# A four-pass recurrent scan on one core: the state update moves from VectorE to ScalarE, with VectorE writing the input line into PSUM ahead of the products

## What is computed

```python
def step(w, b):
    def f(carry, inp):
        nxt = inp + _conv1d(carry, w, b)   # 5 taps, 48 -> 48 channels, along the line
        return (nxt, nxt)
    return f
_, d_rest = scan(step(down_w, down_b), d0, xs[1:])            # D: rows downwards
seq = concatenate([D[Hh - 3::-1], D[Hh - 1:Hh]], 0)
_, u_rest = scan(step(down_w, down_b), u0, seq)               # U: rows upwards, input one line ahead
_, r_rest = scan(step(right_w, right_b), r0, ws[1:])          # R: columns to the right
_, l_rest = scan(step(left_w, left_b), l0, R[Ww - 2::-1])     # L: columns to the left
x = x + L(_gn(x))
```

## Time and profile before

| what | value |
|---|---|
| median of 3 runs | 2966.16 us (2957.53 to 2975.64) |
| the profiled execution, its own time | 2969.76 us |
| its span | 2968.0 us |
| TensorE's granted clock over the span | 0.935 of full |
| TensorE matmul, busy | 2535.7 us (85%) |
| VectorE busy | 1454.5 us (49%) |
| ScalarE busy | 824.4 us (28%) |
| GpSimd busy | 250.2 us (8%) |
| first layer's scan | 980.7 to about 1694 us |
| second layer's scan | about 1797 to 2514 us |

### The profile page before, as it was taken

The page is one execution under the profiler, slowest core; times in us unless marked ns, Lnnn a source line. Parts: engine busy times, 40 slices in busy tenths (PEclk is TensorE's granted clock), DMA queues, the critical chain, the costliest instruction groups (busy, mean ns, idle before and its releaser), DMA issues.

```text
span 2968.0 us, 46070 instructions
## 1 busy us (share of the span) xinstructions
PE 2535.7 (85%) x18068; PEld 2198.1 (74%) x18068; DVE 1454.5 (49%) x3029; ACT 824.4 (28%) x1353; POOL 250.2 (8%) x244
## 2 busy tenths in 40 slices
PE   2989999999999899999999807999999998005786
PEld 2989849849844899999999807999999998002343
DVE  3323233233222555545555674555455556776665
ACT  3433353353356101440024420014400244002221
POOL 1000000000000720000000140000000000344110
PEclk9999999999999899999999958999999999557888
DMA  8830000012002300000000092000000000573222
GB/s 150 148 62 1 1 0 1 1 28 58 1 0 64 65 1 1 1 1 1 1 1 1 12 270 60 1 1 1 1 1 1 1 1 1 178 276 98 85 85 85
DMA packets 51629, 129.81 MB, mean 44 GB/s; under 512 B 9120, under 2 KB 34048, under 8 KB 44896
## 3 DMA queue, kind: packets, MB, share of 16 engines
q1 hardware_dynamic: 48352, 113.92, 15.8%
q10 hardware_dynamic: 2976, 13.34, 1.5%
q0 software_dynamic: 128, 0.01, 0.0%
HBM read 76.91 MB, written 50.33 MB: 43 GB/s over the span
## 4 chain that ended last, share of the span: by engine, by line
PE 83%; DMA 6%; DVE 6%; issue 2%; ACT 1%; POOL 1%; SPq 0%; DVEq 0%; ACTq 0%; POOLq 0%
PE bank L939 18%; PE bank L940 15%; PE bank L941 15%; PE bank L848 13%; PE bank L902 11%; PE bank L863 3%; PE bank L853 3%; DMA flat_rows<-work 2%; PE bank L976 2%; DVE work L316 2%; DMA work<-saved 1%; PE bank L1034 1%; DMA work<-in_x 1%; PE bank L967 1%; DMA saved<-image 1%
## 5 line engine op out<-in xcount | busy, mean ns | idle before, releaser
L1220 DVE SCALAR_TENSOR_TENSOR image<-bank,scan_bias,image 112x128 f32<-112x128 f32 x2032 | 781.8, 385 | 653.3 <-PE bank L941 650.4
L939 PE MATMUL bank<-image,scan_wt 112*112 112x128 f32 x4064 | 852.8, 291 | 32.1 <-ACT image L689 25.5
L940 PE MATMUL bank<-image,scan_wt 112*112 112x126 f32 x4064 | 771.3, 271 | 0.0
L941 PE MATMUL bank<-image,scan_wt 112*112 112x126 f32 x4064 | 770.0, 270 | 0.0
L939 PEld LDWEIGHTS bank<-image,scan_wt 112*112 112x112 f32 x4064 | 557.4, 175 | 65.3 <-ACT image L689 25.7
L940 PEld LDWEIGHTS bank<-image,scan_wt 112*112 112x112 f32 x4064 | 582.5, 176 | 0.0
L941 PEld LDWEIGHTS bank<-image,scan_wt 112*112 112x112 f32 x4064 | 578.8, 176 | 0.0
L848 PE MATMUL bank<-work 112*128 112x192 f32 x2304 | 423.7, 332 | 10.0 <-issue 10.0
L615 ACT ACTIVATE work<-image,gn_shift,gn_scale 48x567 f32<-48x567 f32 (+5 forms) x384 | 332.3, 898 | 345.5 <-PE bank L853 219.3
L707 ACT COPY work<-image 48x256 f32 (+1 forms) x256 | 105.8, 413 | 1041.8 <-PE bank L941 1041.3
L848 PEld LDWEIGHTS bank<-work 112*128 112x128 f32 x2304 | 375.0, 192 | 11.7 <-issue 11.2
(11 more groups left out here) (134 smaller groups left out, 1563.3 us busy)
## 6 DMA issues: line engine op xcount, KB each, us to landing
work<-saved SPq DMA_DIRECT2D x64, 384.0 KB, 8.5
saved<-image SPq DMA_DIRECT2D x10, 1536.0 KB, 20.7
flat_rows<-work ACTq DMA_DIRECT2D x32, 384.0 KB, 7.3
image<-flat_rows SPq DMA_DIRECT2D x4, 3072.0 KB, 13.9
out<-image SPq DMA_DIRECT2D x8, 1536.0 KB, 8.1
saved<-image SPq DMA_DIRECT2D x12, 768.0 KB, 9.5
band<-in_x SPq DMA_DIRECT2D x16, 384.0 KB, 5.5
work<-in_x SPq DMA_DIRECT2D x16, 384.0 KB, 5.5
```

The source lines that it names most:

```text
L939: mm(dst, wt[:, 1], src, start=True, stop=False)
L940: mm(dst[:, 1:J2, :], wt[:, 0], src[:, 0:J2 - 1, :], start=False, stop=False)
L941: mm(dst[:, 0:J2 - 1, :], wt[:, 2], src[:, 1:J2, :], start=False, stop=True).then_inc(s_prod[g], 1)
L1220: v.scalar_tensor_tensor(out=line(g, along_w, at), in0=prod, scalar=scan_bias[:, 3 * layer + kind:3 * layer + kind + 1], in1=line(g, along ...
```

## The change

- Each group now has two PSUM banks, used in turn (`state_bank(g, done)` is `bank[2 * g + done % 2]`).
- VectorE no longer updates the line. One step ahead it writes input line plus bias into the bank of the coming step (`preload`, a `tensor_scalar`), as soon as the state of two steps before has left that bank, and counts up `s_pre[g]`.
- TensorE's three products all have `start=False` and accumulate onto what VectorE wrote. Four products ahead of the first layer (`s_prime`) write the four banks once, so that later ones add.
- ScalarE waits for `s_pre[g]` of the next step and for `s_prod[g]`, copies the 112 x 128 sum from PSUM into the image line (`take_step`) and counts up `s_state[g]`. Its code is unrolled now.
- The exchanges go to VectorE (`swap_part`), single copies put behind the preloads: in passes U and L up to two in a step, three in every two steps, begun 5 or 3 steps late, the rest after the last preload of the pass.
- The counter `s_swap` starts at 0, so the waits for it in GpSimd and TensorE change by one.

```diff
+        def state_bank(g, done):
+            return bank[2 * g + done % 2][0:P, 0:2 * J2].rearrange("p (j q) -> p j q", q=2)
...
@@ scalar
-            def exchange(along_w, i, n):
...
-                own_wait(act, s_swap, n + 1)
-                nc.scalar.copy(swap_tmp[HI], part(LO, 1)).then_inc(s_swap, 1)
-                own_wait(act, s_swap, n + 2)
-                nc.scalar.copy(part(LO, 1), part(HI, 0)).then_inc(s_swap, 1)
-                own_wait(act, s_swap, n + 3)
-                nc.scalar.copy(part(HI, 0), swap_tmp[HI]).then_inc(s_swap, 1)
+            def take_step(layer, done, scan, n):
+                forward, along_w, _, _ = SCANS[scan]
+                _, at = step_at(forward, n)
+                for g in range(2):
+                    if n < STEPS - 1:
+                        act.wait_ge(s_pre[g], layer * PASSES * STEPS + done + 2)
+                    act.wait_ge(s_prod[g], layer * PASSES * STEPS + done + 1)
+                    nc.scalar.copy(line(g, along_w, at), state_bank(g, done)).then_inc(s_state[g], 1)
...
@@ tensor
                 for g in range(2):
+                    if n == 0:
+                        pe.wait_ge(s_pre[g], layer * PASSES * STEPS + done + 1)
                     pe.wait_ge(s_state[g], done + (layer * (PASSES * STEPS + 1) + 1))
                     src = line(g, along_w, at)
-                    dst = bank[g][0:P, 0:2 * J2].rearrange("p (j q) -> p j q", q=2)
-                    mm(dst, wt[:, 1], src, start=True, stop=False)
-                    mm(dst[:, 1:J2, :], wt[:, 0], src[:, 0:J2 - 1, :], start=False, stop=False)
-                    mm(dst[:, 0:J2 - 1, :], wt[:, 2], src[:, 1:J2, :], start=False, stop=True).then_inc(s_prod[g], 1)
+                    dst = state_bank(g, done)
+                    mm(dst, wt[:, 1], src, start=False, stop=False, skip_group_check=True)
+                    mm(dst[:, 1:J2, :], wt[:, 0], src[:, 0:J2 - 1, :], start=False, stop=False,
+                       skip_group_check=True)
+                    mm(dst[:, 0:J2 - 1, :], wt[:, 2], src[:, 1:J2, :], start=False, stop=True,
+                       skip_group_check=True).then_inc(s_prod[g], 1)
+            for i in range(4):
+                if i == 2:
+                    pe.wait_ge(s_sm_v, 5 * NB)
+                mm(bank[i][0:P, 0:2 * J2], group_half[:, :], identp[0:P, 0:2 * J2],
+                   start=True, stop=True).then_inc(s_prime, 1)
...
@@ vector
-            def step(layer, done, scan, n):
...
-                for g in range(2):
-                    dve.wait_ge(s_prod[g], done + (layer * PASSES * STEPS + 1))
-                    prod = bank[g][0:P, 0:2 * J2].rearrange("p (j q) -> p j q", q=2)
-                    v.scalar_tensor_tensor(out=line(g, along_w, at), in0=prod,
-                                           scalar=scan_bias[:, 3 * layer + kind:3 * layer + kind + 1],
-                                           in1=line(g, along_w, src), op0=ALU.add, op1=ALU.add).then_inc(s_state[g], 1)
+            def preload(layer, done, scan, n, g):
...
+                dve.wait_ge(s_state[g], layer * (PASSES * STEPS + 1) + 1 + max(done - 1, 0))
+                v.tensor_scalar(state_bank(g, done), line(g, along_w, src),
+                                scan_bias[:, 3 * layer + kind:3 * layer + kind + 1], None, ALU.add).then_inc(s_pre[g], 1)
+            def swap_part(along_w, i, m, n):
...
+                if n:
+                    dve.wait_ge(s_swap, n)
+                dst, src = ((swap_tmp[HI], part(LO, 1)), (part(LO, 1), part(HI, 0)), (part(HI, 0), swap_tmp[HI]))[m]
+                v.tensor_copy(dst, src).then_inc(s_swap, 1)
...
                 for scan in range(PASSES):
+                    lag = (None, 5, None, 3)[scan]
                     for n in range(STEPS):
-                        step(layer, scan * STEPS + n, scan, n)
+                        for g in range(2):
+                            preload(layer, done + n, scan, n, g)
+                            m = 2 * (n - lag) + g - 1 if lag else -1
+                            if m >= 0 and m % 4 < 3:
+                                swap_part(scan == 3, K2 - 1 - m // 4 - (scan == 1), m % 4, swaps)
+                                swaps += 1
+                    if lag:
+                        for g in range(2):
+                            dve.wait_ge(s_prod[g], layer * PASSES * STEPS + done + STEPS - 1)
+                        for i in ((K2 - 1,) if scan == 1 else ()) + (1,):
+                            for m in range(3):
+                                swap_part(scan == 3, i, m, swaps)
+                                swaps += 1
+                        for g in range(2):
+                            dve.wait_ge(s_state[g], layer * (PASSES * STEPS + 1) + 1 + done + STEPS)
+                        for m in range(3):
+                            swap_part(scan == 3, 0, m, swaps)
+                            swaps += 1
+                        dve.wait_ge(s_swap, swaps)
```

More of the change, by code:

```diff
@@ L249, in build @@
         s_state = [sem(f"s_state{g}") for g in range(2)]
+        s_pre = [sem(f"s_pre{g}") for g in range(2)]
+        s_prime = sem("s_prime")
         s_swap = sem("s_swap")
@@ L514, in _ @@
             pool.wait_ge(s_band, N_BAND)
[L516 removed]
+            pool.wait_ge(s_swap, 6 * K2)
             for g in range(2):
@@ L730, in _ @@
                 last.then_inc(s_tail, 1)
-                for g in range(2):
-                    act.wait_ge(s_prod[g], layer * PASSES * STEPS + 1)
-                n0 = layer * 2 * 3 * K2
-                prod0 = layer * PASSES * STEPS + STEPS
-                with act.Fori(0, K2 - 2) as i:
-                    for g in range(2):
-                        own_wait(act, s_prod[g], 2 * i + (prod0 + 4))
-                    exchange(False, K2 - 2 - i, 3 * i + n0)
-                for g in range(2):
-                    act.wait_ge(s_state[g], layer * (PASSES * STEPS + 1) + 1 + 2 * STEPS)
-                exchange(False, 0, n0 + 3 * (K2 - 2))
-                exchange(False, K2 - 1, n0 + 3 * (K2 - 1))
-                n0 += 3 * K2
-                prod0 += 2 * STEPS
-                with act.Fori(0, K2 - 1) as i:
-                    for g in range(2):
-                        own_wait(act, s_prod[g], 2 * i + (prod0 + 2))
-                    exchange(True, K2 - 1 - i, 3 * i + n0)
-                for g in range(2):
-                    act.wait_ge(s_state[g], (layer + 1) * (PASSES * STEPS + 1))
-                exchange(True, 0, n0 + 3 * (K2 - 1))
+                for scan in range(PASSES):
+                    for n in range(STEPS):
+                        take_step(layer, scan * STEPS + n, scan, n)
             rows = flat.rearrange("b (c n) -> b c n", c=C)
@@ L951, in _ @@
                     if scan == 2:
-                        pe.wait_ge(s_swap, (2 * layer + 1) * 3 * K2 + 1)
+                        pe.wait_ge(s_swap, (2 * layer + 1) * 3 * K2)
                     for n in range(STEPS):
@@ L1216, in step, with part @@
                 src = (at - 1) % H if ahead else at
-                for g in range(2):
-                    dve.wait_ge(s_prod[g], done + (layer * PASSES * STEPS + 1))
-                    prod = bank[g][0:P, 0:2 * J2].rearrange("p (j q) -> p j q", q=2)
-                    v.scalar_tensor_tensor(out=line(g, along_w, at), in0=prod,
-                                           scalar=scan_bias[:, 3 * layer + kind:3 * layer + kind + 1],
-                                           in1=line(g, along_w, src), op0=ALU.add, op1=ALU.add).then_inc(s_state[g], 1)
+                dve.wait_ge(s_state[g], layer * (PASSES * STEPS + 1) + 1 + max(done - 1, 0))
+                v.tensor_scalar(state_bank(g, done), line(g, along_w, src),
+                                scan_bias[:, 3 * layer + kind:3 * layer + kind + 1], None, ALU.add).then_inc(s_pre[g], 1)
+            def swap_part(along_w, i, m, n):
+                def part(rows, s):
+                    return image6[rows, :, s, :, i, :] if along_w else image6[rows, :, s, i, :, :]
+                if n:
+                    dve.wait_ge(s_swap, n)
+                dst, src = ((swap_tmp[HI], part(LO, 1)), (part(LO, 1), part(HI, 0)), (part(HI, 0), swap_tmp[HI]))[m]
+                v.tensor_copy(dst, src).then_inc(s_swap, 1)
             for layer in range(2):
@@ L1268, in _ @@
                 dve.wait_ge(s_scan_c, 16 * N_SCAN_DMA)
+                dve.wait_ge(s_tail, layer + 1)
+                if layer == 0:
+                    dve.wait_ge(s_prime, 4)
+                swaps = layer * 6 * K2
                 for scan in range(PASSES):
+                    done = scan * STEPS
+                    lag = (None, 5, None, 3)[scan]
                     for n in range(STEPS):
-                        step(layer, scan * STEPS + n, scan, n)
-                dve.wait_ge(s_swap, (layer + 1) * 6 * K2 + 1)
-                for g in range(2):
-                    dve.wait_ge(s_state[g], (layer + 1) * (PASSES * STEPS + 1))
```

(3 more changed lines are left out.)

8 lines of the change are left out of this document (2 added, 6 removed).

## The result

The changed kernel takes 2918.6 us (median of 4 runs, 2911.6 to 2925.9), the kernel before 2969.7 us in the same series. The ratio is 0.984, with a 95% interval of 0.982 to 0.986: 1.6% or 48 us faster (the two medians lie 51 us apart). The forecast was 2890 us, a gain of 76 us. The time lies within the range; about 30 us of the expected gain are missing, and the experiments are about them.

What follows compares the result with a forecast made beforehand. The prediction took the latency loop of products, update and hand-over as the bound. From 2969.8 us it took 77 us of shorter steps, giving 2893, then allowed for a profiled run 3.6 us over the median: 2890 us, range 2855 to 2955.

Steps and rivals of the forecast that it cites:

- What bounds the kernel: In the scan, the latency loop of products, update and hand-over sets the step: 1.35 us in U, 1.42 in R.
- The copy in place of the update: In the loop, VectorE's update of 0.35 or 0.42 us becomes a ScalarE copy of 0.27 or 0.30 us.
- The loops are then 0.94 + 0.27 + 0.06: Products, copy and hand-over in the new loop: 1.27 us in D and U, 1.30 in R and L, under TensorE's floor.
- the sum: Forecast saving of all scan steps: 23 us in D and U, 26 in R, 28 in L, 77 us together.
- VectorE's queue: Preloads and exchange copies fit beside two steps: 2.19 us of 2.60 in U, 2.60 of 2.64 in L.
- TensorE's floor: TensorE's own work without waits bounds the new step: 1.30 us in D and U, 1.32 in R and L.
- rivals 1 and 2: VectorE becomes the bound in pass L: 2937 us, chance 0.16; or its queue runs at its dearest: 3001 us, chance 0.07.
- The 0.01 us that L was given for crossings: In pass L, 0.01 us a step added for copies that cross in SBUF, making the step 1.33 us.
- Rival 3: In the loop, ScalarE's copy gains nothing over the update: 2966 us, chance 0.09; if even dearer, 3011 us, chance 0.03.
- The second rule of the Trainium skill: If two-element runs went at full rate, L's preloads and exchange copies would cost 2.19 us in two steps, as in U.
- The border: Between passes U and R, TensorE's idle time falls from 3.29 to about 2 us, a gain of 1 us a layer.
- Rival 4: In all passes the second wait holds the copy, or the preload is late: 2940 to 3000 us, chance 0.05.

Runs made afterwards that it cites:

- e10: The kernel before, with one more, long satisfied wait written ahead of the product's wait on each VectorE update: 3044.4 us, ratio 1.026.
- e9: The changed kernel with the two waits of ScalarE's copy in the other order, product first, preload second: 2887.6 us, ratio 0.972.
- e3: The changed kernel without the exchange copies of passes U and L, except the last of each pass: 2896.3 us, measured once.
- e4: The changed kernel with pass L's exchange copies run between dense scratch lines, same number, size and place in the queue: 2911.9 us, measured once.
- e6: The changed kernel with roles swapped: ScalarE preloads line plus bias and does the exchanges, VectorE copies the sum out: 2955.6 us, ratio 0.997.
- e1: The changed kernel with the wait for the preload moved from ScalarE's copy to TensorE in all steps: 2923.5 us, ratio 0.987.

## Why the prediction was right, and where it missed

**What bounds the kernel.** Right. The loop's sum gave the step before, and e10 shows that it is a loop: what is added to one hand-over comes back in every step.

**The copy in place of the update.** Right. It takes 0.266 us in D and U (forecast 0.27) and 0.299 in R (0.30). Its hand-over to TensorE is 0.05.

**"The loops are then 0.94 + 0.27 + 0.06".** This is the term that was mis-sized. The 0.94 was measured on an update with one wait and carried over to a copy with two; the diff and the order of ScalarE's queue both showed the second, and the prediction priced only what happens if the preload is late. It is 1.01 in R. The loop is therefore 1.36 there and not 1.30, and 1.31 in D and U, just above the floor, so TensorE did not become the bound in the change: its weight load still follows a state by 0.05 us. Against e9, where only the order of the waits differs, that took 508 x 0.016 = 8 us from D and U, 254 x 0.05 = 13 us from R and 254 x 0.04 = 10 us from L. That is 31 of the 34 us by which the steps saved less than the sum had (43 instead of 77). With the waits in the better order the scans lose 76 us. That this is so near to 77 is in part luck, see VectorE's queue below.

**TensorE's floor.** Right: 1.30 and 1.32 were forecast, 1.294 and 1.305 measured.

**VectorE's queue.** The exchange copy was forecast at 0.29 in U and is 0.29, at 0.36 in L and is 0.375 on the mean; the preload at 0.33 and 0.38 and is 0.354 and 0.356 to 0.375. In L the queue is 89% full, but it is not the bound; rivals 1 and 2 didn't happen. The 0.01 us that L was given for crossings should have been 0.05 (e3, e4). That is a term that was mis-sized. With e9's L at 1.369 against a forecast of 1.33, it costs 10 us; e9's lower floors in D and R make up for most of that.

**Rival 3 and the Trainium skill's rule.** By the Trainium skill (VectorE: DVE Perf Modes, TRN2 errata) the two engines' copies of 128 elements from PSUM differ by 0.008 us. Measured, they differ by 0.026 (0.292 and 0.266, e6 and the change), and the update that was replaced took 0.35. So of the 0.084 us that left the loop, 0.058 came from the operation (a plain copy in place of product plus bias plus line) and only 0.026 from the engine. The measurement decides, and the rival fell.

**The second rule of the Trainium skill.** By the Trainium skill (SBUF — State Buffer, Specifications (TRN2)) runs of two fp32 that lie in one 16-byte line are accessed at full rate. The traces agree for the preload, which only reads them (0.354 dense, 0.356 in R of the change). They don't for ScalarE's copy, which writes them (0.266 and 0.299).

**The border.** 2.35 us idle against a forecast of about 2, and 3.29 before: a gain of 0.94 us where 1 was forecast.

**Rival 4** was nearest to the truth in kind, "the second wait holds the copy", but it was meant as a preload that comes late, and it was priced for all passes at a loss.

## What to carry to other kernels

In a loop bound by latency, count the waits in front of each instruction of the loop, not only what they wait for. In these kernels the second of two is an instruction of its own, and when it was the one that ended last, it cost 0.05 to 0.08 us a turn; write first the wait that ends last. A number taken from the old loop (products to update: 0.94 us) is good for the new one only if the instruction at its end is released in the same way.

## What the runs showed of the hardware

- A wait that was satisfied long before cost 77 us in 1016 steps (e10). When it pushes the late wait into an instruction of its own, it costs on VectorE (0.41 to 0.48 or 0.49 us from the last product's start to the operation's, e6 and e10), on ScalarE (0.41 in e9 and e1, 0.46 or 0.47 in the change) and on TensorE (0.05 to 0.12 us from the copy's end to the weight load, e1) alike.
- Strided copies of two engines in SBUF can be stretched where they cross: a ScalarE copy of 0.30 us took 0.344 on the mean beside VectorE's exchange copies and 0.355 beside GpSimd's, and 0.306 beside dense ones. Only every second line pair's copies are long (0.48 to 0.54 us against 0.29 to 0.31). Which resource they share was not tried.
- Fp32 products of 126 to 128 columns went at 1.294 us for twelve passes at the full 2.4 GHz with dense lines, where half of the 2.54 us at 1.2 GHz (twice the 1.27 of the earlier trace rows) would be 1.27; with lines in runs of two it was 1.305. The two clocks don't scale the step exactly.
